# Cross attention over the context: the value product in rounded parts, one normalising half moved to ScalarE, one buffer for the rounded queries

## The chip, the cores and the metric

The kernel runs on one core of a Trainium2 chip. The metric is the device time of one execution in microseconds (us): the median of several. The engines are TensorE (PE in the rows; PEld is its weight load), VectorE (DVE), ScalarE (ACT), GpSimd (POOL) and SyncE (SP, which here issues the transfers). Each runs its own instructions in order and waits for the others through semaphores.

## The reference, cut to what matters

The program is a two-layer decoder on x of 2 x 256 rows and 512 columns: self attention, a small product with the context, a mixing block; then a second attention, **cross attention over 512 context rows per batch**, and a feed-forward block. Only the cross attention changes:

```
H, KVH, HD = (32, 8, 128)
q = (hidden_states @ Wq.T).reshape(bsz, q_len, H, HD).transpose(0, 2, 1, 3)
k = (cross_attention_states @ Wk.T).reshape(bsz, kv_len, KVH, HD).transpose(0, 2, 1, 3)
v = (cross_attention_states @ Wv.T).reshape(bsz, kv_len, KVH, HD).transpose(0, 2, 1, 3)
q = _rmsnorm(q, q_norm_w)
k = _rmsnorm(jnp.repeat(k, GROUPS, axis=1), k_norm_w)
v = jnp.repeat(v, GROUPS, axis=1)
scores = jnp.einsum('bhqd,bhkd->bhqk', q, k) * scale + attention_mask
probs = jax.nn.softmax(scores.astype(jnp.float32), axis=-1)
out = jnp.einsum('bhqk,bhkd->bhqd', probs, v)
return out.transpose(0, 2, 1, 3).reshape(bsz, q_len, H * HD) @ Wo.T
```

## The kernel before, in words

Eight groups (one key/value head and its 4 query heads each) run one after the other. A group has 8 **steps**, s = 0 to 7: step s is batch s // 4 and head s % 4. Keys and values of all groups were computed earlier and lie in DRAM; SP loads a group's ahead.

Many products are made of **rounded parts**: an fp32 operand t is split into high (t rounded, written by ACT) and low (t minus high, written by DVE or POOL), both of the type fp32r, and `product` (L177) issues three matmuls: high by high, low by high, high by low. Scores, query projection and output projection are done so. Three kinds are plain fp32, and each fp32 matmul stands in the trace as two records: the transposes of the probabilities (L1670), the sums of squares of the queries (L1628, one column), and the **value product** (L1684): per step four matmuls of 256 columns, hence eight records.

What TensorE does in step s, in this order: `scores(s)`, six rounded matmuls; `turn_probs(s-1)`, eight records; then 12 rounded matmuls of a query projection (s = 0, 1, 4, 5) or an output projection (s = 2, 3, 6, 7); `turn_keys` in steps 6 and 7; `query_sums` in steps 1, 2, 5, 6; last `values(s-1)`. `query_sums` waits for `x_qlow`, that is until DVE has written the low part of that query head (`query_rest`), since it writes into the bank that `query_rest` reads.

DVE in step s: `logits(s)` (two halves, L1944, then the maximum, L1948), `low(s-2)` (L1965), the step's extra work (`query_rest`, L1924, in steps 1, 2, 5, 6; `add`, L216, in steps 0, 3, 4, 7), `normalise(s)` (reciprocal, L1953, then both halves of the probabilities, L1956), then small or key work (`query_mean`, L1930; `norm_keys`, L1913, in step 5; `keys_rest`, L1918, in steps 6 and 7). ACT in step s: `turned(s-1)` (copies the transposed probabilities out of banks 5 and 6, L1790), `exps(s)` (L1781), rounding of weights (L1595), `query`, `x_squares` or `keys_out` (L1769), and `headed(s-1)` (L1799). POOL makes the low parts of the weights (L1598) and small powers (L1866, L1860). The order is the written order of the code on every engine; no planner moves anything.

Of the kernel before, what the change touches and what calls it, by code (L numbers as in the profile page):

```python
# [14 lines left out]
P = 128  # L15
# [6 lines left out]
HD = 128  # L22
# [13 lines left out]
def decoder_kernel(nc, a, out):  # L36

    sems = {}
    with ExitStack() as ctx:
# [665 lines left out]
        def cross_vector(dve):  # L705
# [6 lines left out]
            def add(t):  # L712
                dve.wait_ge(sem("cross"), t + 1)
                dve.tensor_tensor(x[:, t, :], x[:, t, :], bank[OUT_BANKS[t]][:, :], ALU.add)\
                   .then_inc(sem("cross_added"), 1)

            sums_and_stats(dve, 1, add, "cross_added", 0)
# [863 lines left out]
        def x_load_outputs(sp, g, p):  # L1581
            if due(4 * (g - 1)):
# [4 lines left out]
        q_high = [over(f"q_high{i}", [P, GH, T], f"qT{i}") for i in range(2)]  # L1587
        q_low = [[over(f"q_low{i}{h}", [P, T], host, at) for h, (host, at) in enumerate(homes)]
                 for i, homes in enumerate(((("wkv0", 0), ("wkv0", T * 4), ("wkv1", 0), ("wkv1", T * 4)),
                                            (("tmp6", 0), ("tmp7", 0), ("sig0", 0), ("sig1", 0))))]  # L1590
# [10 lines left out]
        def x_wo_chunk(g, c, last_group):  # L1601

            return KC * (2 * g + (0 if last_group else 1)) + c + 1

        def x_wq_chunk(m, c):

            return c + 1 if isinstance(m, int) and m == 1 else KC * (2 * m - 2) + c + 1
# [5 lines left out]
        def x_tensor(pe):  # L1613
# [18 lines left out]
            def turn_keys(m, p, half_, turned):  # L1632
                pe.wait_ge(sem("x_kn"), 2 * m + half_ + 1)
                if turned is not None:
                    pe.wait_ge(sem("x_turned"), turned)
# [5 lines left out]
            def body(g, p, last_group):  # L1641
# [3 lines left out]
                def scores(s):  # L1645
# [6 lines left out]
                    for c in range(2):  # L1652
# [3 lines left out]
                        product(pe, bank[3 + c][:, :], (q_high[p][:, h, rows_], q_low[p][h][:, rows_]),  # L1656
                                (k_high[p][:, keys_], k_low[p][:, keys_]), True, True).then_inc(sem("x_score"), 1)

                def turn_probs(s):
                    pe.wait_ge(sem("x_norm"), 8 * g + s + 1)  # L1660
                    for half_ in range(2):
                        if due(16 * g + 2 * s + half_ - 1):
                            pe.wait_ge(sem("x_turned"), 16 * g + 2 * s + half_ - 1)
# [93 lines left out]
        def x_scalar(act):  # L1757
            def query(m, p, h):
                act.wait_ge(sem("x_proj"), 4 * m + h + 1)
                if due(16 * (m - 1)):  # L1760
                    act.wait_ge(sem("x_score"), 16 * (m - 1))
                act.activation(q_high[p][:, h, :], bank[h % 2][:, :], ACT.Copy)
                if due(4 * m + h - 1):
                    act.wait_ge(sem("x_qss"), 4 * m + h - 1)
                act.activation(tmp[2 + h % 2][:, :], bank[h % 2][:, :], ACT.Square).then_inc(sem("x_q"), 1)

# [5 lines left out]
            def body(g, p, last_group):  # L1772
# [11 lines left out]

                def turned(s):
                    if due(8 * g + s - 1):
                        act.wait_ge(sem("x_value"), 8 * g + s - 1)
                    for half_ in range(2):
                        act.wait_ge(sem("x_turn"), 16 * g + 2 * s + half_ + 1)
                        act.activation(probT[s % 2][:, 2 * half_:2 * half_ + 2, :].rearrange("p a b -> p (a b)"),  # L1790
# [26 lines left out]
                for s in range(STEPS):  # L1817
                    if s or not first:
                        turned(s - 1)
                    exps(s)  # L1820
                    if first and s in (1, 2):
# [13 lines left out]
                    if s in (2, 3) and not last_group:  # L1835
                        x_squares(act, n, 1 - p, s - 2)
                    if s in (6, 7) and not last_group:
# [9 lines left out]
            for half_ in range(2):  # L1847
                keys_out(0, 0, half_)
            piped_groups(nc.scalar, body)
# [13 lines left out]
        def x_gpsimd(pool):  # L1863
# [4 lines left out]

            def body(g, p, last_group):
# [17 lines left out]
                if not last_group:  # L1887
                    x_key_pow(pool, g + 1)
# [10 lines left out]
            query_pow(0, 0, 1)  # L1899
            piped_groups(nc.gpsimd, body)  # L1900
# [6 lines left out]
        def x_vector(dve):  # L1907
# [14 lines left out]
            def query_rest(m, p, h):  # L1922
                dve.wait_ge(sem("x_q"), 4 * m + h + 1)
                dve.tensor_tensor(q_low[p][h][:, :], bank[h % 2][:, :], q_high[p][:, h, :].bitcast(F32),  # L1924
# [8 lines left out]
            def body(g, p, last_group):  # L1933
# [17 lines left out]
                def normalise(s):  # L1951
# [3 lines left out]
                    for c in range(2):  # L1955
                        last = dve.tensor_scalar(prob[s % 2][:, c, :], prob[s % 2][:, c, :],  # L1956
# [336 lines left out]
```

## Time and profile before

| what | value |
|---|---|
| median of 3 runs | 1529.22 us (1524.73 to 1529.4) |
| the profiled execution | 1526.58 us, its span 1524.6 us |
| mean granted clock of TensorE | 0.976 of full speed |
| PE, PEld busy | 1433.3 us (94%), 1177.7 us (77%) |
| DVE, ACT, POOL busy | 1076.9 (71%), 820.4 (54%), 590.8 us (39%) |
| first and last value matmul of the changed part | 1023.0 and 1479.0 us |

A row of the timeline has the start, the length, the engine, the line of the kernel, the operation with output and inputs, and how many instructions it merges; in square brackets the idle time before it and who ended it. Matmuls are pipelined: their lengths overlap, so what one costs is read from start to start. Group by group the stage repeats; the seven boundaries between groups lie inside the loop.

### The profile page before, as it was taken

The numbers are of one execution on the slowest core, as the hardware profiler recorded it, in microseconds if no ns is written. First come the engines' busy times: TensorE is split into PE (matmuls) and PEld (weight loads), VectorE is DVE, ScalarE is ACT, GpSimd is POOL, SyncE is SP. The second block draws the span as 40 slices with busy tenths as digits, with TensorE's granted clock in tenths as the row PEclk, the third lists the DMA queues.
The fourth block names the chain that finished last, engine by engine and source line by source line (L and its number), as shares of the span: only waits on it lengthen the run. The fifth ranks groups of instructions, "written<-read, shape, count | busy, mean of one in ns | idle before, by whom it ended". The sixth has DMA issues, their size and how long they took to land.

```text
span 1524.6 us, 23524 instructions
## 1 busy us (share of the span) xinstructions
PE 1433.3 (94%) x7314; PEld 1177.7 (77%) x7314; DVE 1076.9 (71%) x2447; ACT 820.4 (54%) x2074; POOL 590.8 (39%) x611
## 2 busy tenths in 40 slices
PE   7999999998899969999999999879999999999986
PEld 6778888876588837787788778668888888888862
DVE  4687667796587968767766776757676676776662
ACT  5656666654212227557655755636556666566440
POOL 3654544531022236557555655424223133132010
PEclk9999999999899969999999999999999999999998
DMA  8011110100323222221321221320201201111000
GB/s 310 1 70 70 70 69 23 46 32 5 148 84 124 83 70 98 97 97 56 116 106 52 99 97 56 124 97 1 84 14 70 80 18 69 46 50 61 1 1 28
DMA packets 30126, 107.65 MB, mean 71 GB/s; under 512 B 3847, under 2 KB 13191, under 8 KB 22104
## 3 DMA queue, kind: packets, MB, share of 16 engines
q1 hardware_dynamic: 30040, 106.58, 19.1%
q8 instruction: 44, 0.72, 0.2%
q14 instruction: 42, 0.34, 0.1%
HBM read 97.07 MB, written 9.50 MB: 70 GB/s over the span
## 4 chain that ended last, share of the span: by engine, by line
PE 56%; issue 17%; DVE 14%; POOL 8%; ACT 3%; POOLq 0%; DMA 0%; DVEq 0%; SPq 0%; ACTq 0%
PE bank L180 11%; PE bank L181 11%; PE bank L182 11%; PE bank L1684 7%; PE bank L1670 3%; POOL yss L1347 2%; PE bank L1628 2%; PE bank L310 2%; POOL tmp L158 1%; PE bank L333 1%; DVE tmp L164 1%; PE bank L1171 1%; DVE q L703 1%; PE bank L279 1%; DVE qT L882 1%
## 5 line engine op out<-in xcount | busy, mean ns | idle before, releaser
L158 POOL TENSOR_TENSOR tmp<-tmp,sin 128x512 f32<-128x512 f32 x80 | 116.0, 1450 | 228.5 <-ACT tmp L151 228.5
L1944 DVE SCALAR_TENSOR_TENSOR logit<-bank,qss,amask 128x512 f32<-128x512 f32 x128 | 91.4, 748 | 86.2 <-PE bank L182 84.9
L182 PE MATMUL bank<-wo_low,att_high 128*128 128x512 f32 x384 | 150.6, 392 | 0.0
L1684 PE MATMUL bank<-probT,v 128*128 128x256 f32 x512 | 123.6, 384 | 1.2 <-ACT probT L1790 1.2
L1866 POOL TENSOR_TENSOR qss<-qss,half 128x4 f32<-128x4 f32 x32 | 34.8, 1089 | 226.9 <-DVE qss L1930 226.9
L1790 ACT ACTIVATE probT<-bank 128x512 f32<-128x512 f32 x128 | 69.5, 595 | 86.2 <-PE bank L1670 86.1
L1781 ACT ACTIVATE prob<-logit,rmax 128x512 f32<-128x512 f32 x128 | 91.5, 716 | 38.7 <-DVE rmax L1948 38.7
L1528 PE MATMUL bank<-kT,wg 128*128 128x256 f32 x512 | 110.9, 379 | 0.5 <-ACT prob L1546 0.5
L1528 PEld LDWEIGHTS bank<-kT,wg 128*128 128x128 f32 x512 | 97.1, 190 | 14.0 <-ACT prob L1546 0.9
L180 PE MATMUL bank<-l_wo_high,att_high 128*128 128x512 f32 x256 | 104.7, 409 | 2.9 <-DVE att_low L571 1.5
L1684 PEld LDWEIGHTS bank<-probT,v 128*128 128x128 f32 x512 | 94.0, 190 | 13.9 <-issue 1.8
L181 PE MATMUL bank<-xT_high,wq_low 128*128 128x512 f32 x256 | 101.9, 398 | 0.0
L149 ACT ACTIVATE tmp<-bank 128x512 f32<-128x512 f32 x80 | 47.3, 592 | 100.5 <-PE bank L182 99.9
L181 PE MATMUL bank<-l_wo_high,att_low 128*128 128x512 f32 x256 | 99.8, 390 | 0.0
L164 DVE TENSOR_TENSOR tmp<-tmp,cos 128x512 f32<-128x512 f32 x80 | 76.1, 952 | 16.9 <-ACT tmp L151 16.8
L420 ACT ACTIVATE prob<-logit,rmax 128x128 f32<-128x128 f32 (+1 forms) x128 | 57.2, 448 | 54.7 <-DVE rmax L553 54.6
L216 DVE TENSOR_TENSOR x<-x,bank 128x512 f32<-128x512 f32 x96 | 64.4, 679 | 29.7 <-PE bank L182 29.6
L182 PEld LDWEIGHTS bank<-wo_low,att_high 128*128 128x128 f32 x384 | 72.1, 188 | 16.8
L1948 DVE TENSOR_REDUCE rmax<-logit 128x2 f32<-128x1024 f32 x64 | 78.1, 1220 | 2.2
L1670 PEld LDWEIGHTS bank<-ident,prob 128*128 128x128 f32 x512 | 59.5, 140 | 13.9 <-DVE prob L1956 5.7
L1670 PE MATMUL bank<-ident,prob 128*128 128x128 f32 x512 | 66.5, 273 | 4.0 <-DVE prob L1956 4.0
L549 DVE TENSOR_TENSOR logit<-bank,keys 128x384 f32<-128x384 f32 x64 | 35.3, 551 | 49.2 <-PE bank L312 49.0
(260 smaller groups left out, 4148.2 us busy)
## 6 DMA issues: line engine op xcount, KB each, us to landing
wq<-in_l_wq SPq DMA_DIRECT2D x16, 1024.0 KB, 5.9
wo<-in_l_wo SPq DMA_DIRECT2D x16, 1024.0 KB, 4.9
wkv<-in_l_wkv SPq DMA_DIRECT2D x16, 512.0 KB, 5.5
wg<-in_l_wg SPq DMA_DIRECT2D x8, 1024.0 KB, 5.0
wq<-in_x_wq SPq DMA_DIRECT2D x8, 1024.0 KB, 7.3
wo<-in_x_wo SPq DMA_DIRECT2D x8, 1024.0 KB, 5.0
kT<-in_x_wkv SPq DMA_DIRECT2D x8, 512.0 KB, 4.4
kv_keys<-logit SPq DMA_DIRECT2D x8, 512.0 KB, 4.8
```

The lines of the kernel that those rows point to most:

```text
L158: eng.tensor_tensor(halves(tmp[4 + j % 2]), halves(tmp[2 + j % 2]), per_batch(sin), ALU.mult).then_inc(sem(f"{l}_sinp"), 1)
L164: eng.tensor_tensor(halves(tmp[j % 2]), halves(tmp[j % 2]), per_batch(cos), ALU.mult).then_inc(sem(f"{l}_cosp"), 1)
L180: eng.matmul(dst, a_high, b_high, start=start, stop=False)
L181: eng.matmul(dst, a_low, b_high, start=False, stop=False)
L182: return eng.matmul(dst, a_high, b_low, start=False, stop=stop)
L1528: last = pe.matmul(bank[KV_BANKS[n % 2]][:, i * 256:(i + 1) * 256], wg[t // CT][:, c, t % CT * P:(t % CT + 1) * P], weights[:, c, :], star ...
L1670: last = pe.transpose(bank[5 + half_][:, kt * L + c * P:kt * L + (c + 1) * P], prob[s % 2][:, c, (2 * half_ + kt) * P:(2 * half_ + kt + 1) ...
L1684: last = pe.matmul(bank[VALUE_BANKS[s % 2]][:, 0:L], v[at][:, b * CT + kt, :], probT[s % 2][:, kt, :], start=(kt == 0), stop=(kt == CT - 1))
L1781: last = act.activation(prob[s % 2][:, c, :], logit[s % 2][:, c, :], ACT.Exp, bias=rmax[s % 2][:, c:c + 1], accum_out=rsum[s % 2][:, c:c + 1])
L1790: act.activation(probT[s % 2][:, 2 * half_:2 * half_ + 2, :].rearrange("p a b -> p (a b)"), bank[5 + half_][:, :], ACT.Copy).then_inc(sem( ...
L1944: dve.scalar_tensor_tensor(logit[s % 2][:, c, :], bank[3 + c][:, :], qss[p][:, 1, h, 2 * b + c:2 * b + c + 1], amask[:, c, :], ALU.mult, A ...
L1948: dve.tensor_reduce(rmax[s % 2][:, 0:2], logit[s % 2][:, :, :], AX.X, ALU.max, negate=True)\
```

## The change

- `values(s)`: instead of four fp32 matmuls, twelve rounded ones of 256 columns: per 128 keys v_high by p_high and v_low by p_high, then four of v_high by p_low. It waits for `x_turned` (p_high) as before, and then also for `x_plow` (p_low).
- ACT writes the transposed probabilities as p_high (fp32r, in the place of probT). DVE gets `probs_rest(s-1)`, right behind `logits(s)`: two instructions of 128x512 that read bank 5 and 6 and write p_low. TensorE may write these banks again only after `x_plow`.
- `normalise(s)`: DVE scales the first half, ACT the second, both after DVE's reciprocal; `x_norm` is counted twice.
- The values are split: `high_values` on ACT in steps 2 and 3 for the next group (two copies of 128x512), `low_values` on POOL (two subtractions, in place).
- `q_high` and `q_low` have one buffer instead of two; the wait on `x_score` is set head by head. The space goes to p_low and v_high.
- Counters of `x_split` and `x_high` are renumbered, and two semaphores elsewhere share one name (`rows_added`).

```diff
                 def values(s):
                     at, b, h = x_step(p, s)
                     if s == 0:
-                        pe.wait_ge(sem(f"x_values{p}"), 8 * (g - p) + 16)
+                        pe.wait_ge(sem("x_split"), x_v_chunk(g, 1))
...
+                    dst = bank[VALUE_BANKS[s % 2]][:, 0:L]
                     for kt in range(CT):
                         if kt % 2 == 0:
                             pe.wait_ge(sem("x_turned"), 16 * g + 2 * s + kt // 2 + 1)
-                        last = pe.matmul(bank[VALUE_BANKS[s % 2]][:, 0:L], v[at][:, b * CT + kt, :],
-                                         probT[s % 2][:, kt, :], start=(kt == 0), stop=(kt == CT - 1))
+                        pe.matmul(dst, v_high[at][:, b * CT + kt, :], p_high[s % 2][:, kt, :],
+                                  start=(kt == 0), stop=False)
+                        pe.matmul(dst, v_low[at][:, b * CT + kt, :], p_high[s % 2][:, kt, :], start=False, stop=False)
+                    for kt in range(CT):
+                        if kt % 2 == 0:
+                            pe.wait_ge(sem("x_plow"), 16 * g + 2 * s + kt // 2 + 1)
+                        last = pe.matmul(dst, v_high[at][:, b * CT + kt, :], p_low[s % 2][:, kt, :],
+                                         start=False, stop=(kt == CT - 1))
                     last.then_inc(sem("x_value"), 1)
...
             def query(m, p, h):
                 act.wait_ge(sem("x_proj"), 4 * m + h + 1)
-                if due(16 * (m - 1)):
-                    act.wait_ge(sem("x_score"), 16 * (m - 1))
-                act.activation(q_high[p][:, h, :], bank[h % 2][:, :], ACT.Copy)
+                if due(16 * (m - 1) + 2 * (GH + h) + 2):
+                    act.wait_ge(sem("x_score"), 16 * (m - 1) + 2 * (GH + h) + 2)
+                act.activation(q_high[:, h, :], bank[h % 2][:, :], ACT.Copy)
...
+            def high_values(m, p, half_):
+                if half_ == 0:
+                    act.wait_ge(sem(f"x_values{p}"), 8 * (m - p) + 16)
+                act.activation(v_half(v_high[p], half_), v_half(v[p], half_), ACT.Copy).then_inc(sem("x_high"), 1)
...
+                def normalise(s):
+                    act.wait_ge(sem("recip"), STEPS * NG + 8 * g + s + 1)
+                    act.activation(prob[s % 2][:, 1, :], prob[s % 2][:, 1, :], ACT.Copy,
+                                   scale=rsum[s % 2][:, 3:4]).then_inc(sem("x_norm"), 1)
...
                     exps(s)
+                    normalise(s)
...
+            def low_values(m, p):
+                for half_ in range(2):
+                    pool.wait_ge(sem("x_high"), x_v_chunk(m, half_))
+                    pool.tensor_tensor(v_half(v_low[p], half_), v_half(v[p], half_),
+                                       v_half(v_high[p], half_).bitcast(F32), ALU.subtract)\
+                        .then_inc(sem("x_split"), 1)
...
+                def probs_rest(s):
+                    for half_ in range(2):
+                        dve.wait_ge(sem("x_turned"), 16 * g + 2 * s + half_ + 1)
+                        at = (slice(None), slice(2 * half_, 2 * half_ + 2), slice(None))
+                        dve.tensor_tensor(p_low[s % 2][at].rearrange("p a b -> p (a b)"), bank[5 + half_][:, :],
+                                          p_high[s % 2][at].rearrange("p a b -> p (a b)").bitcast(F32),
+                                          ALU.subtract).then_inc(sem("x_plow"), 1)
...
                 for s in range(STEPS):
                     logits(s)
+                    if s or not first:
+                        probs_rest(s - 1)
                     if s >= 2 or not first:
                         low(s - 2)
```

DVE in step 5 of the first group, before (q_low_87 is the low part of the next group's first query head):

```order
1212 L1944 SCALAR_TENSOR_TENSOR logit<-bank,qss,amask 128x512 [waits x_score,x_exp,x_qrms]
1213 L1944 SCALAR_TENSOR_TENSOR logit<-bank,qss,amask 128x512 [waits x_score]
1214 L1948 TENSOR_REDUCE rmax<-logit 128x2 [waits x_scaled]
1215 L1965 TENSOR_TENSOR att_low<-bank,att_high 128x256 [waits x_headed]
1216 L1924 TENSOR_TENSOR q_low_87<-bank,q_high_82 128x512 [waits x_q]
1217 L1953 RECIPROCAL rsum<-rsum 128x2 [waits x_exp]
1218 L1956 TENSOR_SCALAR prob<-prob,rsum 128x512 [waits recip]
1219 L1956 TENSOR_SCALAR prob<-prob,rsum 128x512
```

The same place after the change:

```order
1211 L1983 SCALAR_TENSOR_TENSOR logit<-bank,qss,amask 128x512 [waits x_score,x_exp,x_qrms]
1212 L1983 SCALAR_TENSOR_TENSOR logit<-bank,qss,amask 128x512 [waits x_score]
1213 L1987 TENSOR_REDUCE rmax<-logit 128x2 [waits x_scaled]
1214 L2001 TENSOR_TENSOR p_low_88<-bank,p_high_86 128x512 [waits x_turned] x2
1215 L2010 TENSOR_TENSOR att_low<-bank,att_high 128x256 [waits x_headed]
1216 L1963 TENSOR_TENSOR q_low_82<-bank,q_high 128x512 [waits x_q]
1217 L1992 RECIPROCAL rsum<-rsum 128x2 [waits x_exp]
1218 L1994 TENSOR_SCALAR prob<-prob,rsum 128x512 [waits recip]
```

Two instructions of 128x512 now stand between the maximum and the query's low part, and one instruction of 128x512 behind the reciprocal is gone.

## Rows read from the trace of the kernel before

**Rows 1.** The page, busy time of each engine over the whole span

```profile
PE 1433.3 (94%) x7314; PEld 1177.7 (77%) x7314; DVE 1076.9 (71%) x2447; ACT 820.4 (54%) x2074; POOL 590.8 (39%) x611
```

**Rows 2.** Windows of 60 us: busy time of each engine, granted clock, DMA

```profile
1180.00:1240.00 60.00, 60.00 (x319) 51.25 (x318) 42.55 (x76) 36.35 (x92) 16.26 (x13) 1.00 0.15 54
```

**Rows 3.** Waits of PE from 1030 to 1460 us: total, times, longest

```profile
PE bank L1670 <- DVE prob L1956: 1.4, 2, 1.2
```

**Rows 4.** Timeline of PE, one step 3 and the start of the next step

```profile
1206.42 0.58 PE L180 MATMUL bank<-k_high,q_high 128*128 128x512 f32 x1
...
1208.80 0.47 PE L180 MATMUL bank<-wo_high,att_high 128*128 128x512 f32 x1
1209.11 0.39 PE L181 MATMUL bank<-wo_high,att_low 128*128 128x512 f32 x1
...
1211.43 0.39 PE L182 MATMUL bank<-wo_low,att_high 128*128 128x512 f32 x1
1211.66 1.89 PE L1684 MATMUL bank<-probT,v 128*128 128x256 f32 x8
1213.19 0.58 PE L180 MATMUL bank<-k_high,q_high 128*128 128x512 f32 x1
1213.61 0.39 PE L181 MATMUL bank<-k_high,q_low 128*128 128x512 f32 x1
```

**Rows 5.** Timeline of PE in the stage before, fp32 matmuls of 128 columns

```profile
880.12 1.95 PE L1125 MATMUL bank<-wkv,xT 128*128 128x128 f32 x16
881.82 0.47 PE L180 MATMUL bank<-l_wo_high,att_high 128*128 128x512 f32 x1
882.13 0.39 PE L181 MATMUL bank<-l_wo_high,att_low 128*128 128x512 f32 x1
```

**Rows 6.** Timeline of PE, step 5: first scores, and the query sums

```profile
1219.96 0.58 PE L180 MATMUL bank<-k_high,q_high 128*128 128x512 f32 x1
...
1225.19 0.95 PE L1628 MATMUL bank<-ones,tmp 128*128 128x1 f32 x8
```

**Rows 7.** Timeline of DVE, end of step 4 and step 5

```profile
1217.21 0.68 DVE L216 TENSOR_TENSOR x<-x,bank 128x512 f32<-128x512 f32 x1
1217.81 0.17 DVE L1904 TENSOR_SCALAR kss<-kss 128x8 f32<-128x8 f32 x1
...
1221.04 1.45 DVE L1944 SCALAR_TENSOR_TENSOR logit<-bank,qss,amask 128x512 f32<-128x512 f32 x2 [1.39 <-PE bank L182]
1222.51 1.22 DVE L1948 TENSOR_REDUCE rmax<-logit 128x2 f32<-128x1024 f32 x1
...
1223.98 0.68 DVE L1924 TENSOR_TENSOR q_low<-bank,q_high 128x512 fp32r<-128x512 f32 x1
1225.32 0.17 DVE L1953 RECIPROCAL rsum<-rsum 128x2 f32<-128x2 f32 x1 [0.66 <-ACT prob L1781]
```

**Rows 8.** Timeline at the stage's start, DVE and PE: query sums that wait

```profile
1009.81 0.69 DVE L1924 TENSOR_TENSOR q_low<-bank,q_high 128x512 fp32r<-128x512 f32 x1 [2.10 <-ACT tmp L1765]
...
1010.56 1.05 PE L1628 MATMUL bank<-ones,tmp 128*128 128x1 f32 x8 [0.24 <-DVE q_low L1924]
...
1011.47 0.49 PE L180 MATMUL bank<-k_high,q_high 128*128 128x512 f32 x1
```

**Rows 9.** Timeline of PE, step 6: the query sums

```profile
1233.30 0.95 PE L1628 MATMUL bank<-ones,tmp 128*128 128x1 f32 x8
```

**Rows 10.** Timeline of DVE, step 6: low part of a query head

```profile
1231.65 0.68 DVE L1924 TENSOR_TENSOR q_low<-bank,q_high 128x512 fp32r<-128x512 f32 x1
```

**Rows 11.** Timeline of PE, the first scores of step 0

```profile
1242.94 0.58 PE L180 MATMUL bank<-k_high,q_high 128*128 128x512 f32 x1
```

**Rows 12.** Timeline of ACT, step 7: weights rounded, keys out

```profile
1240.97 1.14 ACT L1595 ACTIVATE wq_high<-wq 128x512 fp32r<-128x512 f32 x2
1242.01 0.67 ACT L1769 ACTIVATE k_high<-bank,dvec 128x512 fp32r<-128x512 f32 x1
```

**Rows 13.** Timeline of DVE, step 7: low part of the keys

```profile
1243.14 0.74 DVE L1918 SCALAR_TENSOR_TENSOR k_low<-bank,dvec,k_high 128x512 fp32r<-128x512 f32 x1
```

More of the change, by code:

```diff
@@ L714, in add @@
                 dve.tensor_tensor(x[:, t, :], x[:, t, :], bank[OUT_BANKS[t]][:, :], ALU.add)\
-                   .then_inc(sem("cross_added"), 1)
-            sums_and_stats(dve, 1, add, "cross_added", 0)
+                   .then_inc(sem("rows_added"), 1)
+            sums_and_stats(dve, 1, add, "rows_added", 0)
         def cross_tensor(pe):
@@ L1586, in decoder_kernel @@
         VALUE_BANKS = [2, 7]
[L1587 to L1590, printed above, removed]
+        q_high = over("q_high", [P, GH, T], "qT0")
+        q_low = [over(f"q_low{h}", [P, T], f"wkv{h // 2}", h % 2 * T * 4) for h in range(GH)]
+        p_high = [over(f"p_high{i}", [P, CT, L], f"probT{i}") for i in range(2)]
+        p_low = [over(f"p_low{i}", [P, CT, L], "qT1", i * CT * L * 4) for i in range(2)]
+        v_high = [over(f"v_high{i}", [P, B * CT, HD], host) for i, host in enumerate(("tmp6", "sig0"))]
+        v_low = [over(f"v_low{i}", [P, B * CT, HD], f"v{i}") for i in range(2)]
         k_high = [over(f"k_high{i}", [P, B * C], f"kT{i}") for i in range(2)]
@@ L1601, in x_wo_chunk, with x_v_chunk, v_half @@
         def x_wo_chunk(g, c, last_group):
-            return KC * (2 * g + (0 if last_group else 1)) + c + 1
+            return 2 + (2 * KC + 2) * g + (0 if last_group else KC + 2) + c + 1
         def x_wq_chunk(m, c):
-            return c + 1 if isinstance(m, int) and m == 1 else KC * (2 * m - 2) + c + 1
+            return 2 + c + 1 if isinstance(m, int) and m == 1 else 2 + (2 * KC + 2) * (m - 1) + c + 1
+        def x_v_chunk(m, c):
+            return c + 1 if isinstance(m, int) and m == 0 else 2 + KC + (2 * KC + 2) * (m - 1) + c + 1
+        def v_half(t, c):
+            return t[:, c * CT:(c + 1) * CT, :].rearrange("p t d -> p (t d)")
         def x_step(p, s):
@@ L1923, in query_rest @@
                 dve.wait_ge(sem("x_q"), 4 * m + h + 1)
-                dve.tensor_tensor(q_low[p][h][:, :], bank[h % 2][:, :], q_high[p][:, h, :].bitcast(F32),
+                dve.tensor_tensor(q_low[h][:, :], bank[h % 2][:, :], q_high[:, h, :].bitcast(F32),
                                   ALU.subtract).then_inc(sem("x_qlow"), 1)
@@ L1954, in normalise @@
                     dve.wait_ge(sem("recip"), STEPS * NG + 8 * g + s + 1)
-                    for c in range(2):
-                        last = dve.tensor_scalar(prob[s % 2][:, c, :], prob[s % 2][:, c, :],
-                                                 rsum[s % 2][:, 2 + c:3 + c], None, ALU.mult)
-                    last.then_inc(sem("x_norm"), 1)
+                    dve.tensor_scalar(prob[s % 2][:, 0, :], prob[s % 2][:, 0, :], rsum[s % 2][:, 2:3], None,
+                                      ALU.mult).then_inc(sem("x_norm"), 1)
+                def probs_rest(s):
+                    for half_ in range(2):
+                        dve.wait_ge(sem("x_turned"), 16 * g + 2 * s + half_ + 1)
[3 more added lines that the diff above has]
+                                          ALU.subtract).then_inc(sem("x_plow"), 1)
                 def low(s):
@@ L1996, in body @@
                 if last_group:
+                    probs_rest(7)
                     low(6)
@@ L2054, in add @@
                 dve.tensor_tensor(x[:, t, :], x[:, t, :], bank[OUT_BANKS[t]][:, :], ALU.add)\
-                   .then_inc(sem("ffn_added"), 1)
-            sums_and_stats(dve, 5, add, "ffn_added", 0)
+                   .then_inc(sem("rows_added"), 1)
+            sums_and_stats(dve, 5, add, "rows_added", NT)
         block = ctx.enter_context(nc.Block())
```

14 lines of the change are left out of this document (9 added, 5 removed).

## The prediction, made before the changed kernel ran

> **What bounds the kernel now.** I read the busy times first, then the windows of the changed stage, then the waits of TensorE in it, then the timelines of one group on TensorE, DVE and ACT. Over the span TensorE is busy 94% [rows 1]. In the cross attention it is busy the whole window at the full clock (1.00 of 2.4 GHz), while DVE has 42.6 us of 60, ACT 36.4 and POOL 16.3 [rows 2]. TensorE's waits for the probabilities come to 1.4 us in 430 us [rows 3]. So the stage, whose first scores start at 1011.47 [rows 8] and which ends at about 1482, lasts as long as TensorE's list of matmuls, and two things count: what the new matmuls cost from start to start, and whether any wait grows beyond the room it has. The rest of the program is the same; the renamed semaphores and counters I cost at nothing, as they issue no work.
>
> **The value product: what is removed.** In a step 3 the rounded matmuls of 512 columns are spaced (1211.43 - 1209.11) / 10 = 0.232 us. The eight fp32 records take 1213.19 - 1211.66 = 1.53 us to the next start, and the next matmul comes 0.42 us later instead of 0.23, so 0.19 us of them is still in the pipe: 1.72 us in all [rows 4]. That is 0.215 us for each record, which for 256 columns streamed twice (0.213 us at 2.4 GHz) leaves almost nothing over.
>
> **What is added.** Twelve rounded matmuls of 256 columns. No row shows a rounded matmul with fewer than 512 columns, so I bound it. A rounded one of 512 columns takes 0.232 us where streaming needs 0.213, 0.019 us more. If this is a fixed adder, 256 columns cost 0.107 + 0.019 = 0.126 us, and the twelve 1.51 us. The cheapest that the trace supports is an fp32 record with a weight load of 128 columns behind 128 columns streamed twice: (1.70 + 0.08) / 16 = 0.111 us [rows 5], the same streamed time as 256 columns once; twelve are 1.34 us. The dearest is that the rounded stream is bound by its weight load, not by its columns: then they stay at 0.232 us and cost 2.79 us. I take 0.126, the adder seen in the nearest row. TensorE's own saving is then 1.72 - 1.51 = 0.21 us a step, over 64 steps **-13.6 us**; with the ends -24.5 us (0.38 a step) and +68 us (1.07 a step).
>
> The Trainium skill has a rule for this spacing: "TensorE: Matmul & The Clock Gate", section "Back-to-back issue gap", gives a warm gap of columns / 2.4 GHz plus 2.5 ns for matmuls back to back. The trace agrees for the fp32 records (0.215) and not for the rounded ones of 512 columns (0.232 measured, 0.216 by the rule). An estimate from that page would be 12 x 0.109 = 1.31 us, a saving of 0.41 us a step and 26 us in all.
>
> **DVE: the wait that is new.** `probs_rest` puts two instructions in front of the low part of the query. Each reads a bank and an SBUF tile of 128x512, as `add` and `query_rest` do: 0.68 us long, and 1217.81 - 1217.21 = 0.60 us from one start to the next [rows 7]. They come behind the maximum, which ends at the same offset from the scores as before, since it hangs on the scores alone. So `query_rest` ends 1.20 us later. Before, it ends at 1223.98 + 0.68 = 1224.66 [rows 7], and the query sums start at 1225.19, 5.23 us behind the first scores of the step [rows 6]. Afterwards it ends at 1225.86; a start that waited came 0.06 us behind the release (1010.50 to 1010.56) [rows 8]: 1225.92. **TensorE stands still for 0.73 us.** Starting from standstill also costs: the block that waited is 1.05 us long, the same block without a wait 0.95 [rows 6, 8]; so 0.83 us in all. Nothing else on TensorE can fill this: the value product stands behind the query sums. In steps 1, 2 and 5 the sums stand at this place. In step 6 `turn_keys` stands ahead: sums at 1233.30, low part ready at 1231.65 + 0.68 + 1.20 + 0.06 = 1233.59 [rows 9, 10], so 0.29 + 0.10 = 0.39 us. Counting: step 1 in seven groups, step 2 in eight, step 5 in seven, 22 x 0.83 = 18.3; the first group's step 1, where the stage is still starting, about 0.6; step 6 in seven, 2.7. **+21.6 us.**
>
> **The rest of the chain in a step.** The reciprocal moves from 1225.32 [rows 7] to 1223.98 + 1.20 + 0.60 = 1225.78, 0.46 us; DVE then scales one half instead of two, ACT the other beside it (a copy of 128x512 takes it about 0.57 us from start to start [rows 12]). Both halves are done at 1225.78 + 0.20 + 0.57 = 1226.6, 6.6 us behind the step's first scores at 1219.96, and the transposes need them behind the next step's six score matmuls, at over 8: hidden. p_low is complete at 1222.51 + 1.14 + 1.28 = 1224.9, 5.0 us behind them, and the value product, which starts behind a projection of 2.8 us, asks for it after 6: hidden. On DVE the change adds 2 x 0.60 and removes about 0.44 us a step, 0.76 us; it is idle 17.4 of 60 us [rows 2], which is 2.1 of a step of 7.2 (456 us between the first and the last value matmul, 63 steps): it doesn't become the bound as a sum, only at this one place.
>
> **ACT and the end of a group.** In step 7 ACT's list moves back by the later reciprocal (0.46), its distance (0.3) and the half it now scales (0.57), about 1.3 us. The keys' rounding moves from 1242.01 [rows 12] to 1243.3, ends at 1244.0, and `keys_rest` on DVE ends at 1244.8 instead of 1243.14 + 0.74 = 1243.88 [rows 13]. TensorE wants it for the second half of the transposes of step 0, which is six score matmuls, what was left in the pipe and the first half, 1.39 + 0.19 + 0.44 = 2.0 us behind the first scores at 1242.94 - 0.21 [rows 11], that is 1244.7. A wait of 0.1 to 0.3 with its restart, seven times: **+1.5 us**. DVE is then about 1 us late into step 0, has no query head in it, and catches up. The two copies of values on ACT (1.1 us a group) fall in steps 2 and 3, and POOL's two subtractions beside 16 of 60 us [rows 2]: nothing. The one buffer for the queries waits only for scores that stand ahead of the projection on TensorE: nothing.
>
> **The sum.** 1526.6 - 13.6 + 21.6 + 1.5 = 1536.1 us against the profiled execution, which lies 2.6 us under the median and inside the runs (1524.7 to 1529.4). I say **1537 us**, slower by about 0.6%. A difference under 0.3% (4.6 us) can't be told from none here.
>
> **The rivals.**
> - *The rounded stream is tight at 256 columns.* At 0.111 us TensorE saves 24.5 us and the waits eat 23.1: 1525 us, no change. For it: nothing says that the adder of 0.019 belongs to the matmul and not to its columns (in proportion it would be 0.116). Against: fp32 records of the same stage have no such adder, so something fixed to the rounded kind is there.
> - *The query sums don't wait as I work it out.* The mechanism stands at one place, the distance of 0.53 us between 1224.66 and 1225.19 [rows 6, 7]. If the two DVE instructions delay the low part by less than that, the wait is gone and the saving stays: 1526.6 - 13.6 + 1.5 = 1514 us, with the tight stream 1504. It decides below 0.27 us an instruction; nothing in the rows is as short as this for 128x512 from a bank. A mixture, half the wait and a tight stream, is 1514 too. This is the rival on the other side.
> - *The weight load bounds the rounded stream.* 1526.6 + 68 + 23 = 1618 us. For it: each rounded load starts with the matmul before it and 0.232 isn't explained by the columns. Against: fp32 loads of the same 128x128 follow each other at 0.111 us [rows 5].
> - *DVE or ACT late through a whole group.* If the lateness of step 7 doesn't fade before step 1, `query_rest` ends up to 1 us later there and in the steps behind: about 1 us more a group, 1545 us.
>
> There is a reckoning on the page "FP8 and Floating Point Precision", section "TensorE Precision Notes", of the Trainium skill: true fp32 takes four passes. Three products are three passes, so an estimate from it alone is a quarter off 1.72 us, 0.43 a step or 27 us, and with my waits 1523 us; it belongs to the first rival and doesn't change its chance.
>
> **How the numbers follow.** Forecast 0.47 (1537), tight stream 0.23 (1525), no or half a wait 0.16 (1504 to 1518), late engines 0.08 (1545), weight load 0.06 (1618). The range reaches from 1519 to 1547: it leaves out the weight load and most of the missing wait. The likeliest case's own range is 1530 to 1543. Slower by over 0.3%: most of the forecast, late engines, weight load, and a little of the first rival, 0.57; within 0.3%: 0.26; faster 0.17.
>
> **What would show it.** The value product's starts at 0.126 us (or 0.111, or 0.232). In the waits of TensorE a new first row: the query sums waiting for the low part of the query, some 30 times, 0.3 to 0.8 us each, 18 us in all, and a small one of the transposes waiting for the keys' low part. A step 3, 6.77 us from scores to scores [rows 4], shorter by 0.21, a step 5 longer by 0.6. I am wrong if the query sums wait under 5 us in total, if TensorE waits longer for the probabilities or for p_low, or if anything outside 1000 to 1500 us changes length.

## The result, and the profile after

| | before | after |
|---|---|---|
| median of the timed runs | 1529.31 us (1524.73 to 1530.96, 4 runs) | 1540.41 us (1538.94 to 1540.89, 4 runs) |
| span of the profiled execution | 1524.6 us | 1538.9 us |
| mean granted clock, of 2.4 GHz | 0.976 | 0.972 |

The ratio is 1.0076, with the interval 1.0053 to 1.0099: slower by 0.8%. Forecast was 1537 us (range 1519 to 1547), which is 0.5% over 1529.2, though the prediction calls it about 0.6%.

The page after, busy time of each engine over the span, answers to [rows 1]:

```profile
PE 1432.6 (93%) x7570; PEld 1177.9 (77%) x7570; DVE 1117.7 (73%) x2511; ACT 869.3 (56%) x2154; POOL 609.3 (40%) x627
```

TensorE has 256 more records and 0.7 us less busy time. DVE has 41 us more, ACT 49 us more. The same 60 us as in [rows 2], after:

```profile
1180.00:1240.00 60.00, 58.03 (x349) 49.55 (x348) 46.50 (x83) 41.98 (x102) 18.72 (x15) 1.00 0.14 54
```

TensorE, which had no gap there, now stands still for 2 us of 60, while the busiest of the others, DVE, has 46.5: no other engine has become the bound as a sum. Who is waited for stands in the waits of TensorE from 1030 to 1500 us (total, times, longest):

```profile
PE bank L1637 <- DVE q_low L1963: 16.2, 25, 3.4
PE bank L1694 <- ACT p_high L1816: 2.1, 3, 1.3
PE bank L180 <- DVE att_low L2010: 2.1, 1, 2.1
PE bank L1679 <- DVE k_low L1957: 0.8, 4, 0.2
PE bank L180 <- POOL wo_low L1600: 0.6, 1, 0.6
PE bank L1700 <- DVE p_low L2001: 0.6, 2, 0.3
```

Before, the same window has two rows inside the stage, for the probabilities and their transposes, and none for `q_low` ([rows 3] ends at 1460 us and leaves out the second of its two rows):

```profile
PE bank L1670 <- DVE prob L1956: 2.9, 3, 1.4
PE bank L1684 <- ACT probT L1790: 1.2, 3, 0.4
```

The first row after is the forecast wait: the query sums (L1637) for the low part of a query head. Counted from 1000 us, with those of the stage's start, it is 16.7 us in 27 waits: 21 of 0.54 to 0.63 us, five of 0.18 to 0.26, and one of 3.4.

**Both terms in one step.** The timeline of DVE in a step 1 answers to [rows 7]: the two instructions of `probs_rest` (L2001) and the low part of the attention (L2010) stand ahead of `q_low`.

```profile
1199.51 1.22 DVE L1987 TENSOR_REDUCE rmax<-logit 128x2 f32<-128x1024 f32 x1
1200.64 1.28 DVE L2001 TENSOR_TENSOR p_low<-bank,p_high 128x512 fp32r<-128x512 f32 x2
1201.84 0.42 DVE L2010 TENSOR_TENSOR att_low<-bank,att_high 128x256 fp32r<-128x256 f32 x1
1202.17 0.68 DVE L1963 TENSOR_TENSOR q_low<-bank,q_high 128x512 fp32r<-128x512 f32 x1
```

`q_low` ends at 1202.85, and the timeline of TensorE in the same step answers to [rows 6]:

```profile
1197.11 0.40 PE L180 MATMUL bank<-k_high,q_high 128*128 128x512 f32 x1
...
1202.91 1.05 PE L1637 MATMUL bank<-ones,tmp 128*128 128x1 f32 x8 [0.56 <-DVE q_low L1963]
1203.82 0.36 PE L1694 MATMUL bank<-p_high,v_high 128*128 128x256 f32 x1
1204.02 0.28 PE L1696 MATMUL bank<-p_high,v_low 128*128 128x256 f32 x1
```

The sums start 5.80 us behind the first scores instead of 5.23, so they are 0.57 us late; they are 0.06 us behind the end of `q_low`, and the block is 1.05 us long as forecast for a start from standstill. Part of the value product's saving already lies ahead of this point (the second scores come 0.23 us behind the first, not 0.42), so the delay is larger than 0.57; the first experiment gives it. The first value matmul behind the sums takes 0.20 us instead of 0.12, but it does so in that experiment as well, where nothing waits.

A step 3 has no wait; its value product, in the timeline of TensorE, answers to the eight fp32 records of [rows 4]:

```profile
1218.62 0.28 PE L1694 MATMUL bank<-p_high,v_high 128*128 128x256 f32 x1
1218.74 0.28 PE L1696 MATMUL bank<-p_high,v_low 128*128 128x256 f32 x1
...
1219.58 0.63 PE L1700 MATMUL bank<-p_low,v_high 128*128 128x256 f32 x4
1220.04 0.40 PE L180 MATMUL bank<-k_high,q_high 128*128 128x512 f32 x1
```

Twelve starts take 1220.04 - 1218.62 = 1.42 us, 0.118 each. Against 1.72 us before this is 0.30 a step.

**Where the 14.3 us of span come from.** From the starts of the first scores of each step, in us:

| step of a middle group | 0 | 1 | 2 | 3 | 4 | 5 | 6 | 7 | group |
|---|---|---|---|---|---|---|---|---|---|
| before | 6.79 | 7.67 | 7.68 | 6.77 | 6.77 | 7.66 | 8.11 | 7.21 | 58.7 |
| after | 6.87 | 8.23 | 8.21 | 6.49 | 6.48 | 8.20 | 8.18 | 6.91 | 59.6 |

Steps 3, 4 and 7 gain 0.28 to 0.30; step 0, which has no query sums either, loses 0.08; steps 1, 2 and 5 lose 0.53 to 0.56 net; step 6 loses 0.07. The six middle groups give +5.8 us and the last group -0.5. The remainder lies at three places: +0.8 us ahead of the stage, +3.1 us in the first group (55.4 to 58.4), and +5.1 us from the last step's scores to the end (57.4 to 62.5). I had costed the last two at little or nothing. The +0.8 us arises ahead of 1003 us, where the work is the same. In the changed kernel and its five variants below, which don't differ there at all, the first scores start anywhere from 1010.8 to 1014.1 us, so 0.8 us can't be put down to the change.

*The first group.* In its step 2 there is no output projection yet, so little stands between the scores and the sums. The wait is the longest of all, and the granted clock falls behind it. Timeline of TensorE, then the windows from 1024 us (PE, PEld, DVE, ACT and POOL busy, granted clock, DMA share, GB/s), after:

```profile
1031.54 1.05 PE L1637 MATMUL bank<-ones,tmp 128*128 128x1 f32 x8 [3.41 <-DVE q_low L1963]
```

```profile
1032.00:1036.00 4.00, 4.00 (x21) 3.81 (x21) 0.24 (x2) 3.42 (x13) 3.13 (x3) 0.57 0.02 4
1036.00:1040.00 4.00, 3.30 (x22) 2.67 (x21) 3.48 (x5) 1.91 (x5) 1.61 (x2) 1.00 0.01 2
```

Before, that wait was 2.21 us, and from 1030 to 1038 the clock was 1.00:

```profile
1029.42 1.05 PE L1628 MATMUL bank<-ones,tmp 128*128 128x1 f32 x8 [2.21 <-DVE q_low L1924]
```

*The tail.* The last output projection (L180) waits for `att_low` of step 6, as TensorE's timeline shows:

```profile
1485.96 0.47 PE L180 MATMUL bank<-wo_high,att_high 128*128 128x512 f32 x1 [2.06 <-DVE att_low L2010]
```

DVE's timeline there tells why: `att_low` (`low(6)` in the program) is written behind `probs_rest(7)`, and that waits for ACT to round the last probabilities.

```profile
1481.84 0.49 DVE L1994 TENSOR_SCALAR prob<-prob,rsum 128x512 f32<-128x512 f32 x1
1484.19 1.29 DVE L2001 TENSOR_TENSOR p_low<-bank,p_high 128x512 fp32r<-128x512 f32 x2 [1.86 <-ACT p_high L1816]
1485.40 0.42 DVE L2010 TENSOR_TENSOR att_low<-bank,att_high 128x256 fp32r<-128x256 f32 x1
```

Again the clock falls behind the wait (windows, same columns); at the corresponding place before, 1480 to 1484, it was 1.00:

```profile
1486.00:1490.00 4.00, 4.00 (x12) 3.23 (x13) 0.00 (x0) 0.00 (x0) 0.00 (x0) 0.57 0.00 0
```

And one block behind the stage, which the change doesn't touch, runs longer. The timelines of TensorE, before and then after:

```profile
1493.62 3.60 PE L2024 MATMUL bank<-xT,loraA 128*48 128x512 f32 x8 [0.78 <-ACT xT L688]
```

```profile
1505.54 6.02 PE L2072 MATMUL bank<-xT,loraA 128*48 128x512 f32 x8 [0.78 <-ACT xT L688]
```

### The profile page after: what moved, and what is told of

Its sections match the earlier page's. It is cut to its first block, busy times and chain, and to the rows that moved or that the text cites. A ratio compares the mean times of both kernels' runs of the same rounds, so it can differ in the third digit from the quotient of the medians.

```text
span 1538.9 us, 24206 instructions
## 1 busy us (share of the span) xinstructions
PE 1432.6 (93%) x7570; PEld 1177.9 (77%) x7570; DVE 1117.7 (73%) x2511; ACT 869.3 (56%) x2154; POOL 609.3 (40%) x627
## 4 chain that ended last, share of the span: by engine, by line
PE 43%; DVE 25%; issue 18%; POOL 8%; ACT 4%; POOLq 0%; DMA 0%; DVEq 0%; SPq 0%; ACTq 0%
PE bank L180 8%; PE bank L182 8%; PE bank L181 8%; DVE p_low L2001 3%; DVE logit L1983 3%; DVE rmax L1987 3%; PE bank L1637 2%; POOL yss L1347 2%; PE bank L1694 2%; PE bank L1700 2%; PE bank L1696 2%; POOL tmp L158 1%; DVE tmp L164 1%; PE bank L310 1%; PE bank L1171 1%
## 5 line engine op out<-in xcount | busy, mean ns | idle before, releaser
L180 PE MATMUL bank<-l_wo_high,att_high 128*128 128x512 f32 x256 | 104.6, 409 | 2.9 <-DVE att_low L571 1.5
L1816 ACT ACTIVATE p_high<-bank 128x512 fp32r<-128x512 f32 x128 | 70.1, 597 | 54.9 <-PE bank L1679 54.4
L164 DVE TENSOR_TENSOR tmp<-tmp,cos 128x512 f32<-128x512 f32 x80 | 76.2, 952 | 16.9 <-ACT tmp L151 16.8
L182 PEld LDWEIGHTS bank<-wo_low,att_high 128*128 128x128 f32 x384 | 72.3, 188 | 16.7
L2001 DVE TENSOR_TENSOR p_low<-bank,p_high 128x512 fp32r<-128x512 f32 x128 | 81.8, 681 | 1.9 <-ACT p_high L1816 1.9
L1694 PE MATMUL bank<-p_high,v_high 128*128 128x256 f32 x256 | 68.0, 297 | 2.1 <-ACT p_high L1816 2.1
L1679 PE MATMUL bank<-ident,prob 128*128 128x128 f32 x512 | 67.6, 273 | 2.0 <-ACT prob L1808 1.0
L1679 PEld LDWEIGHTS bank<-ident,prob 128*128 128x128 f32 x512 | 59.4, 140 | 12.4 <-ACT prob L1808 1.7
```

Of the source, the lines that this page charges most:

```text
L164: eng.tensor_tensor(halves(tmp[j % 2]), halves(tmp[j % 2]), per_batch(cos), ALU.mult).then_inc(sem(f"{l}_cosp"), 1)
L180: eng.matmul(dst, a_high, b_high, start=start, stop=False)
L182: return eng.matmul(dst, a_high, b_low, start=False, stop=stop)
L1679: last = pe.transpose(bank[5 + half_][:, kt * L + c * P:kt * L + (c + 1) * P], prob[s % 2][:, c, (2 * half_ + kt) * P:(2 * half_ + kt + 1) ...
L1694: pe.matmul(dst, v_high[at][:, b * CT + kt, :], p_high[s % 2][:, kt, :], start=(kt == 0), stop=False)
L2001: dve.tensor_tensor(p_low[s % 2][at].rearrange("p a b -> p (a b)"), bank[5 + half_][:, :], p_high[s % 2][at].rearrange("p a b -> p (a b)") ...
```

## The experiments

The theory: the rounded product is cheaper by 0.28 to 0.30 us a step, but two DVE instructions placed ahead of the low part of the query make TensorE wait, with a smaller loss of the same kind in the tail. The rivals: the time is lost to something else that the change adds (ACT's half, the traffic of the value product beside DVE), or DVE's greater load itself is the cause and no order of its list helps.

**The query's low part first.** Only the place of two calls in DVE's list is changed:

```
                     logits(s)
+                    if s in (1, 2):
+                        query_rest(g, p, s + 1)
+                    if s in (5, 6) and not last_group:
+                        query_rest(n, 1 - p, s - 5)
                     if s or not first:
                         probs_rest(s - 1)
```

(and the same four lines deleted further down)

> The changed kernel with one thing moved: in steps 1, 2, 5 and 6 VectorE writes the query's low part right behind the maximum, ahead of the two instructions that write the probabilities' low part. Nothing is added or taken away. If the loss is the wait of the query sums in VectorE's queue, that wait falls from 16.7 us to under 3, a step 5 goes from 8.20 us back to 7.66 - 0.28 = 7.4, a group from 59.6 to 56.5 us, and the time to about 1540 - 23 = 1517 us, 0.99 of the kernel before. If the loss is something else that the added work brings (VectorE or ScalarE too full, slower matmuls), the order changes nothing: 1540 us, and the same time appears as a wait for the probabilities' low part or for the probabilities. The tail behind the last group keeps its 2 us wait and its slow clock.

Measured: 1515.16 us (1514.29 to 1517.28), ratio to the kernel before 0.9914 [0.9890, 0.9939]. The steps are 6.95, 7.39, 7.39, 6.49, 6.47, 7.38, 7.83 and 6.94 us, a group 56.8. The wait for `q_low` is down to 2.1 us in 2 waits; what is left of waits in the groups is small. TensorE's waits from 1030 to 1500 us, which takes in the end of the program, too:

```profile
PE bank L1694 <- ACT p_high L1816: 2.8, 3, 1.3
PE bank L180 <- DVE att_low L2010: 2.1, 1, 2.1
PE bank L1679 <- DVE k_low L1957: 1.4, 6, 0.3
```

A step 5 of this kernel shows the sums without a wait, in the timelines of TensorE and of DVE:

```profile
1212.94 0.40 PE L180 MATMUL bank<-k_high,q_high 128*128 128x512 f32 x1
1217.99 0.95 PE L1637 MATMUL bank<-ones,tmp 128*128 128x1 f32 x8
```

```profile
1216.44 0.68 DVE L1963 TENSOR_TENSOR q_low<-bank,q_high 128x512 fp32r<-128x512 f32 x1
```

They start 5.05 us behind the first scores, 0.87 us behind the end of `q_low`. With the wait it was 5.80. So the wait delays TensorE by 0.74 us (mean of steps 1, 2 and 5 of the six middle groups), and the block itself is 0.10 shorter without it.

The first group, too, is shorter (53.6 us), and the clock stays at 1.00 from 1028 to 1040. All of the change's work is still done, `p_low` and ACT's half included; only the order on DVE is another. So it was the order that cost 25 us, not the load. The rest of the stage's cost is the keys: step 0 is 0.16 us longer than before (6.95 to 6.79) where the saving would have made it 0.28 shorter. The six waits for `k_low` (L1679) stand there, one in the step 0 of each middle group.

**The tail alone.**

```
                 if last_group:
-                    probs_rest(7)
                     low(6)
+                    probs_rest(7)
                     low(7)
```

> The changed kernel with one thing moved: behind the last group VectorE writes the low part of head 6's output ahead of the last probabilities' low part, not behind it. If the tail's loss comes from this order, TensorE's wait of 2.1 us there falls to under 0.5, the granted clock behind it stays at 1.00 instead of 0.57, and the time is 4 us (at most 5) under that of the changed kernel, 1536. If the slow clock there falls by chance with the place of the idle time, the wait goes but the stretch of 6 us at 0.59 before the feed-forward block stays: 2 to 3 us under, 1538.

Measured: 1535.82 us (1531.39 to 1540.46, 10 runs), ratio 1.0045 [1.0028, 1.0062]. The wait is gone, and the clock in the window that had 0.57 is 1.00:

```profile
1484.00:1490.00 6.00, 6.00 (x34) 5.11 (x33) 3.18 (x6) 0.52 (x2) 0.00 (x0) 1.00 0.00 0
```

The median is 4.6 us lower, but these ten runs spread over 9 us. The traces say it more exactly: from the last step's scores to the end it is 59.0 us instead of 62.5. So a wait of 2.1 us cost 3.5, which includes the slow clock behind it; 62.5 against 59.0 is also the difference of the tails between the first experiment and the next one. The block of the low-rank product stays at 6.00 us, so that isn't a consequence of this wait.

**Both moves.**

> Both moves together, the query's low part first in steps 1, 2, 5, 6 and the output's low part first in the tail. If the two losses are apart, they add: 1540 - 23 - 4 = 1513 us, about 0.99 of the kernel before, which is the saving of the value product alone (64 x 0.28 = 18 us under 1529, less a wait for the keys' low part). If they are one (all of it VectorE's fullness) it is no better than the first move alone.

Measured: 1511.66 us (1510.84 to 1514.13), ratio 0.9888 [0.9866, 0.9911]. This is the fastest kernel of the study, 17.9 us under the one before by the medians. In the traces its span is 12.5 us shorter (1512.1 to 1524.6): the start of the stage is 1.3 us later, the low-rank block 2.4 us longer, so the stage itself 16.2 us shorter, out of 64 x 0.28 = 18 that its matmuls save. What is missing goes mostly to step 0, the keys.

**The kernel before, with DVE work at the same place.** If two DVE instructions ahead of the query are enough, then the old kernel with nothing but such work must get the same wait. One instruction over 128x1024, whose result nobody reads, is put ahead of the query in every step but the first:

```
                     logits(s)
+                    if s or not first:
+                        dve.tensor_tensor(spare[:, :, :], logit[s % 2][:, :, :], amask[:, :, :], ALU.subtract)
```

> The kernel before, with one added VectorE instruction per step behind the maximum: logits minus mask, 128x1024, into a spare place that nobody reads, about 1.2 us from start to start, as long as the two added ones. The value product stays fp32, ScalarE and GpSimd get nothing. If VectorE's queue ahead of the query's low part is what costs, this alone gives the wait of the query sums (about 0.7 us in steps 1, 2, 5, 0.3 in step 6) and 20 to 24 us: 1551 us, 1.015 of the kernel before. If the loss needs the rounded product or the work on ScalarE, it is within 3 us of 1529, as VectorE is idle 17 of 60 us.

Measured: 1566.29 us (1564.94 to 1567.9), ratio 1.0251 [1.0227, 1.0275]. The wait appears, in the waits of TensorE from 1030 to 1500 us:

```profile
PE bank L1629 <- DVE q_low L1925: 16.0, 21, 1.4
PE bank L1671 <- DVE prob L1957: 2.8, 2, 2.6
PE bank L1685 <- ACT probT L1791: 0.8, 2, 0.4
```

Steps 1 and 2 become 8.44 us, longer by 0.76 as expected, so the mechanism is confirmed with the old value product in place. The size is off: 38 us of span where 20 to 24 were expected. The largest part of the excess is step 5, which grows by 1.5 to 2.8 us (2.28 in the group shown, 13.4 in six); step 6 grows by 0.8 and step 0 by 0.5, and the first and last group give 9.7 us together. In step 5 DVE's timeline shows the added instruction at 2.02 us while POOL computes `wo_low` (3.81 us from 1237.35). Of the 63 added instructions 56 take 1.22 us; the seven that take 1.60 to 2.02 are just those that run beside `wo_low`. TensorE's timeline there shows a wait of 1.30 us instead of 0.52:

```profile
1240.21 2.02 DVE L1975 TENSOR_TENSOR spare<-logit,amask 128x1024 bf16<-128x1024 f32 x1
```

```profile
1243.22 1.05 PE L1629 MATMUL bank<-ones,tmp 128*128 128x1 f32 x8 [1.30 <-DVE q_low L1925]
```

```profile
1244.50:1248.00 3.50, 3.50 (x11) 2.85 (x10) 1.20 (x2) 0.38 (x1) 2.65 (x2) 0.58 0.00 0
```

The last row, a window, shows the clock behind it at 0.58; before it was 1.00 there. Of the six middle groups four have this slow clock behind the wait in step 5 and two have not, with waits of 1.26 to 1.36 us in all six. Steps 5 and 6 together take 19.3 to 19.4 us with it and 17.7 to 17.8 without: the slow clock costs 1.6 us. My expectation had neither.

**The sums behind the value product.** The other cure for the wait: TensorE does the value product first and asks for `q_low` later.

```
+                    if s or not first:
+                        values(s - 1)
                     if s in (1, 2):
                         query_sums(g, s + 1)
                     if s in (5, 6) and not last_group:
                         query_sums(n, s - 5)
-                    if s or not first:
-                        values(s - 1)
```

> The changed kernel with VectorE's order left alone and TensorE's changed: in steps 1, 2, 5 and 6 the value product comes ahead of the query sums. If the loss is that nothing on TensorE stood between the projection and the sums, the 1.42 us of the value product now cover the 0.72 us of wait: steps 1 and 2 go from 8.2 to 7.4 us, the wait of the sums from 16.7 to under 4 us. VectorE gets the sums 1.4 us later, still ahead of its next logits in steps 1, 2, 6, about 0.5 us late in step 5, where the keys' scaling follows. Time 1518 us, between 1515 and 1524. If the delay on VectorE costs wherever it is taken (VectorE the bound), this order helps nothing: 1540 us.

Measured: 1522.02 us (1518.11 to 1523.46, 7 runs), ratio 0.9952 [0.9935, 0.9969], inside the expected range. The waits for `q_low` are down to 0.7 us, but in TensorE's waits from 1030 to 1500 us stands another:

```profile
PE bank L180 <- POOL wo_low L1600: 5.8, 8, 0.9
```

The query sums, now 1.4 us later, feed a small POOL instruction on `qss`, and on POOL the rounding of the output weights is queued behind it. POOL's timeline, then TensorE's at the projection that needs them (step 6, which takes 8.94 us instead of 7.83):

```profile
1224.37 1.42 POOL L1896 TENSOR_TENSOR qss<-qss,half 128x4 f32<-128x4 f32 x1 [2.89 <-DVE qss L1969]
1225.76 1.27 POOL L1600 TENSOR_TENSOR wo_low<-wo,wo_high 128x512 fp32r<-128x512 f32 x1
```

```profile
1227.35 0.47 PE L180 MATMUL bank<-wo_high,att_high 128*128 128x512 f32 x1 [0.90 <-POOL wo_low L1600]
```

A group is 57.7 us, 0.9 more than with the query's low part first. So the same wait can be taken away on the other engine as well, but what hangs on the later result moves back with it.

**Both halves on DVE.** The best version with DVE scaling both halves and ACT none, to see what the half on ACT is worth:

```
-                def normalise(s):
-                    act.wait_ge(sem("recip"), STEPS * NG + 8 * g + s + 1)
-                    act.activation(prob[s % 2][:, 1, :], ...
...
-                    dve.tensor_scalar(prob[s % 2][:, 0, :], ...
+                    for c in range(2):
+                        dve.tensor_scalar(prob[s % 2][:, c, :], ...
```

> The version with both moves (1511.7 us), and the second half of the probabilities scaled by VectorE again, as before the change; ScalarE loses that instruction. If half of the scaling on ScalarE is off the path, VectorE's 0.44 us more a step are hidden as well (transposes ask for the probabilities over 1 us later), ScalarE's keys come earlier and the wait of 1.4 us for the keys' low part goes: 1509 to 1513 us. If VectorE needed the relief, TensorE's wait for the probabilities grows in 64 steps by up to 0.4 us: 1520 to 1537 us.

Measured: 1516.63 us (1514.15 to 1518.78), ratio 0.9919 [0.9894, 0.9943], 5.0 us above the best version: between the two expectations. Where POOL is idle, DVE's list takes the second half without a wait of TensorE. But in the last step of a group both halves take 2.94 us on DVE instead of 0.88, since POOL rounds `wq` at this time. The timelines of DVE, of POOL and of TensorE:

```profile
1239.05 2.94 DVE L1989 TENSOR_SCALAR prob<-prob,rsum 128x512 f32<-128x512 f32 x2
...
1247.45 0.89 DVE L1989 TENSOR_SCALAR prob<-prob,rsum 128x512 f32<-128x512 f32 x2
```

```profile
1238.98 2.73 POOL L1600 TENSOR_TENSOR wq_low<-wq,wq_high 128x512 fp32r<-128x512 f32 x2 [3.34 <-ACT wq_high L1597]
```

```profile
1242.12 1.24 PE L1679 MATMUL bank<-ident,prob 128*128 128x128 f32 x8 [0.43 <-DVE prob L1989]
```

Six such waits and what follows them make a middle group 57.34 instead of 56.83 us, 3.1 us over six. The last group adds 2.3 (there a wait for the probabilities is 2.0 us), the other 1.7 are in the start of the stage (1.3, within what it varies by anyway) and the first group, and the low-rank block at full clock gives 2.4 back: 4.7 us between the spans of the two profiled executions. The half on ACT is thus worth something, though not where a step as a whole would lead one to look.

## Why the prediction came out, step by step

**The value product: right in sign, mis-sized.** I took the 0.019 us that a rounded matmul of 512 columns has above its streaming as a fixed adder, and got 0.126 us and -13.6 us. It measures 0.118, near the value in proportion to the columns (0.116), which I had named and given to the tight-stream rival. From scores to scores a step gains 0.28 us, 64 times, so -18 us, of which the kernel with both moves keeps 16. So the term was 4 us too small. The rival bound by the weight load is out.

**The wait of the query sums: right.** The form (some 30 waits forecast, 27 found, a new first row), its places and its size in a step hold. Forecast were 0.73 + 0.10 = 0.83 us in steps 1, 2 and 5; against the kernel with the query first, 0.74 + 0.10 are measured, and against the kernel before, 0.53 to 0.56 net of the 0.28 saved. (The maximum doesn't keep its offset from the scores, as I had said; it starts 2.40 us behind them instead of 2.58. But the unhindered sums move forward by as much, so the difference holds.) Step 6 was forecast at 0.39 and measures 0.07 to 0.10 net, so 0.35 to 0.38. The first kernel of the experiments takes the wait away by order alone, the fourth makes it in the old kernel. The rival without the wait falls.

**Keys and the end of a group: right in kind, a little small.** +1.5 us were forecast for `k_low`, seven times 0.2. It comes six times, since the last group's step 0 has no such wait, and each time step 0 falls short of its saving by 0.36 us: 2.2 us. The view of the waits lists four of them, 0.8 us. ACT's scaling is 0.72 us long and 0.63 from start to start, where I took 0.57 from a plain copy; it is hidden but for these waits, as are `p_low` (681 ns each; TensorE waits 0.6 us for it in all) and the rounding of the values.

**Edges and clock: missed.** I costed the first group like the others but for 0.6 us in its step 1, which gives it about +1 us, and the tail at nothing. Trace and code would have shown both: in the first group's step 2 the sums waited 2.21 us already before the change, so that DVE's 1.2 us count in full (this wait ends at 1029.42, just ahead of the window of [rows 3]); and in the tail `low(6)` is written behind `probs_rest(7)`, which waits for ACT. And I had not reckoned with the clock, which fell behind both waits. The edges are +3.1 and +5.1 us. The 5.1 are 3.5 for the tail's wait with its clock and 2.4 in the low-rank block, less 0.8 that the tail saves elsewhere. One of my signs of being wrong came true by this: lengths outside 1000 to 1500 us changed, by 0.8 us ahead of the stage and by 2.4 us in the low-rank block, which lies at 1505.5 us after.

**The sum again, from measured terms.** The six middle groups: -13.4 (48 steps x 0.28), +16.9 (six times 3 x 0.82 + 0.35) and +2.2 (six times 0.36) are +5.7, where 5.8 was measured and 8.5 forecast for them (-10.1, +17.3, +1.3). Then +3.1 for the first group, -0.5 for the last, +5.1 for the tail and +0.8 ahead of the stage: 14.3, where 9.5 were forecast. (The medians moved by 11.1 only, as the profiled execution of the kernel before lies 2.7 us under its median.) The saving that I took too small and the edges that I left out have opposite signs, and this is why 1537 lies so near to 1540. That is luck: with the right saving and the rest of my sum as it stands, 1526.6 - 17.9 + 21.6 + 1.5, I would have said 1532. The mechanism and the sign of the result are right; 3 us of nearness are not to its credit.

**What stays open.** The low-rank block takes 6.0 us in the changed kernel and in the first three experiments, and 3.60 in the kernel before and in the last three. The difference is the granted clock, 0.5 against 1.00, at its start; TensorE stands still for 6.35 us one block ahead in all of them. Neither an order nor a wait that I changed goes with it: the third and the sixth kernel have the same order in the tail and differ. It is 2.4 us of the 5.1 in the tail, seen in one profile of each kernel, and I can't put a cause to it. It need not belong to the kernel at all: 13 executions of the kernel before have spans from 1522.5 to 1531.6 us, with mean granted clocks from 0.978 down to 0.971, so the same program differs from one execution to the next by more than this block. For the same reason the slow clock behind the tail's wait, found in two of the three kernels that have this wait, isn't shown to be a property of its kernel.

## What to carry to other kernels

Before an instruction is put into an engine's list, look for what is queued behind it at that place and how much room its consumer has: here 1.2 us of DVE work, with DVE idle more than a quarter of the time, cost more than the product on TensorE saved, and four moved lines turned a loss of 0.8% into a gain of 0.9%, and a fifth made it 1.1%. Walk through the first and the last round of a loop by themselves, since they lack the work that hides a delay in the middle. And when a result is made later, follow all that hangs on it in the other engines' queues.

## What the hardware showed that I had not expected

- A rounded matmul of 256 columns is spaced at 0.118 us and one of 512 at 0.232: about 1.1 times the streaming at 2.4 GHz for both (0.011 and 0.019 us on top), so what comes on top grows with the columns and is no fixed adder. By the rule that the prediction cited (Trainium skill, "TensorE: Matmul & The Clock Gate", section "Back-to-back issue gap") it would be 0.109; the trace disagrees for rounded matmuls of both widths.
- Behind 21 TensorE waits of 0.54 to 0.63 us in the changed kernel the granted clock stayed at 1.00. Behind its waits of 3.4 and 2.1 us it was 0.57 over the next 4 us, that is mostly the lower of its two levels, 1.2 GHz; the two other kernels with a wait of 3.4 us show the same behind it. But the length of one wait alone doesn't decide it. No clock was lost behind 2.21 us in the first group of the kernel before, behind 1.89 us at the same place with the query's low part first, or behind 1.31 us for `p_high` in the last group of the changed kernel. Of six waits of 1.26 to 1.36 us at the same place of six groups, in the kernel with the added DVE work, four were followed by the slow clock and two were not. And the tail's wait of 2.1 us cost 3.5 us in the changed kernel but only 1.8 us, without the slow clock, in the kernel with the sums behind the value product (a tail of 58.4 us against 59.0 - 2.4 without wait, both with the low-rank block at full clock). So what a wait beyond a microsecond costs can double.
- Some DVE instructions with all operands in SBUF were stretched while POOL ran a tensor instruction over 128x512: 128x1024 with two sources from 1.22 to 2.02 us, two scalings of 128x512 from 0.88 to 2.94. The kernel before has it already: there the two scalings of a step 7 take 1.92 us (from 1241.30). Beside the same kind of POOL work `p_low`, with one source in a bank, stayed at 0.68 us, and the maximum over 128x1024 in SBUF, with one source, at 1.22. The page "Advanced Engine Details and Errata" of the Trainium skill, section "GPSIMD Details", states that POOL shares a read and a write interface with DVE, and names two SBUF inputs and the two-port modes as what conflicts. The instruction with two sources and the two that weren't stretched agree with it; a scaling has one source, so it agrees only if it runs in a two-port mode, which no row here shows.
